# Linear attention with a folded FFN on one core: three transposes taken off TensorE

## What is computed

```python
q = _split_heads(x @ Wq.T + bq); k = _split_heads(x @ Wk.T + bk); v = _split_heads(x @ Wv.T + bv)
q = jnp.exp(q)
k = jnp.exp(k)
kv = jnp.cumsum(k[:, :, :, None] * v[:, :, None, :], axis=1)
k1 = jnp.cumsum(k, axis=1)
num = jnp.einsum('zsD,zsDd->zsd', q, kv)
den = jnp.sum(q * k1, axis=-1, keepdims=True)
att = merge_heads(num / den) @ Wo.T + bo
x1 = _layernorm(x + att)
h = x1 @ weight @ aux_weight1 @ aux_weight2
out = _layernorm(x1 + jnp.tanh(h + bias))
```

## Time and profile before

| | us |
|---|---|
| median of 3 runs | 2523.06 |
| lowest, highest | 2522.86, 2527.0 |
| the profiled execution | 2528.05 |
| its span, first to last instruction | 2526.3 |

### The profile page before, as it was taken

The page is one execution under the profiler, slowest core; times in us unless marked ns, Lnnn a source line. Parts: engine busy times, 40 slices in busy tenths (PEclk is TensorE's granted clock), DMA queues, the critical chain, the costliest instruction groups (busy, mean ns, idle before and its releaser), DMA issues.

```text
span 2526.3 us, 58437 instructions
## 1 busy us (share of the span) xinstructions
PE 2459.0 (97%) x22544; PEld 2082.3 (82%) x22544; DVE 1545.7 (61%) x2459; ACT 1070.2 (42%) x2156; POOL 1174.9 (47%) x1543
## 2 busy tenths in 40 slices
PE   7999999999999999999999999999999999999986
PEld 6788888888888888888888888888888888888875
DVE  4666656666566566656656666665665666666564
ACT  3434434444444444444444344444444444444432
POOL 0445444544454454444445445444544444454554
PEclk9999999999999999999999999999999999999997
DMA  4111111111111111111111111111111111111100
GB/s 158 39 45 45 39 42 48 39 39 51 39 39 43 47 39 39 51 39 38 47 43 39 41 49 39 39 50 40 39 43 47 39 39 47 43 38 43 35 30 26
DMA packets 59930, 111.99 MB, mean 44 GB/s; under 512 B 6720, under 2 KB 6720, under 8 KB 59712
## 3 DMA queue, kind: packets, MB, share of 16 engines
q1 hardware_dynamic: 59712, 108.56, 13.6%
HBM read 74.98 MB, written 33.55 MB: 43 GB/s over the span
## 4 chain that ended last, share of the span: by engine, by line
PE 96%; issue 2%; DVE 1%; ACT 0%; DMA 0%; POOL 0%; POOLq 0%; DVEq 0%; SPq 0%
PE G L273 19%; PE G L274 18%; PE G L275 18%; PE SC L340 6%; PE G L352 5%; PE SC L275 5%; PE SC L273 5%; PE SC L274 5%; PE G L329 4%; PE G L441 2%; PE G L424 2%; PE G L432 2%; PE G L361 1%; PE G L375 1%; PE G L376 1%
## 5 line engine op out<-in xcount | busy, mean ns | idle before, releaser
L721 POOL TENSOR_SCALAR_AFFINE_SELECT A<-A 128x512 f32<-128x512 f32 x512 | 313.8, 636 | 306.1 <-ACT A L495 306.1
L648 DVE RECIPROCAL o<-G 128x512 f32<-128x512 f32 x128 | 428.4, 3347 | 5.3 <-PE G L376 3.0
L495 ACT ACTIVATE A<-SC 128x512 f32<-128x512 f32 x512 | 278.5, 601 | 298.2 <-PE G L352 294.9
L530 ACT ACTIVATE QT<-G,bcol 128x512 f32<-128x512 f32 x128 | 88.3, 690 | 591.9 <-PE G L275 591.9
L755 POOL TENSOR_TENSOR qk1L<-WK,qk1H 128x512 fp32r<-128x512 f32 x128 | 163.2, 1275 | 342.4 <-ACT qk1H L535 342.4
L743 POOL TENSOR_SCALAR ve<-mv 128x1 f32<-128x1 f32 x128 | 28.5, 223 | 623.5 <-DVE mv L671 623.5
L643 DVE TENSOR_TENSOR WK<-G,bfbc 128x512 f32<-128x512 f32 x128 | 88.7, 693 | 300.1 <-PE G L275 300.1
L696 DVE TENSOR_TENSOR xTL<-G,xTH 128x512 fp32r<-128x512 f32 x128 | 88.5, 692 | 217.9 <-ACT xTH L543 217.8
L273 PE MATMUL G<-WfH,x1H 128*128 128x512 f32 x512 | 215.1, 420 | 1.6 <-DVE x1L L629 1.5
L635 DVE TENSOR_TENSOR o<-G,o 128x512 f32<-128x512 f32 x128 | 88.5, 692 | 196.0 <-PE G L352 195.9
L273 PE MATMUL G<-xTH,WkH 128*128 128x512 f32 x512 | 202.0, 394 | 5.9 <-DVE WkL L584 5.9
(11 more groups left out here) (113 smaller groups left out, 5747.1 us busy)
## 6 DMA issues: line engine op xcount, KB each, us to landing
xin<-x SPq DMA_DIRECT2D x128, 256.0 KB, 2.7
xres<-x SPq DMA_DIRECT2D x128, 256.0 KB, 2.6
out<-WK SPq DMA_DIRECT2D x128, 256.0 KB, 2.0
QT<-wqT SPq DMA_DIRECT2D x1, 1024.0 KB, 5.6
KT<-wkT SPq DMA_DIRECT2D x1, 1024.0 KB, 6.8
A<-a1T SPq DMA_DIRECT2D x1, 1024.0 KB, 7.8
WK<-a SPq DMA_DIRECT2D x1, 1024.0 KB, 10.0
WK<-wT SPq DMA_DIRECT2D x1, 1024.0 KB, 12.1
```

Source lines behind the costliest of these rows:

```text
L495: nc.scalar.activation(A[:, j, :, :].rearrange("p g q -> p (g q)"), SC[:, j, :], ACT.Copy).then_inc(scores_out[j], 1)
L648: nc.vector.reciprocal(oflat, den_ps[:, :]).then_inc(recip_ready, 1)
L721: last = nc.gpsimd.affine_select(out=A[:, j, :, :], in_=A[:, j, :, :], compare_op=ALU.is_ge, fill=0.0, base=0, pattern=[[0, NK], [1, P]], ...
```

## The change

The three transposes leave TensorE. For each, VectorE turns the 32x32 blocks of the 128x512 tile where they stand (`nc.vector.transpose`), and transfers put the blocks in their places. The identity matrix and the PSUM banks for the transposes go away.

- x: its load is now four transfers of 32 partitions each, which place the blocks at the load (`x_b`), and VectorE turns the blocks in place at the end of slot k for tile k+8. ScalarE makes xTH from that. The subtraction for xTL is now made by GpSimd, for tile k+7 in slot k, after the masks.
- K: VectorE turns the blocks into KS after the reciprocal, SyncE stores KS into a scratch tensor in device memory (`k_rows`), waits for it to land and loads Ktok back in four transfers.
- x1: SyncE stores x1 into a scratch tensor (`x1_rows`) and loads x1s back in four transfers; in the next slot VectorE turns the blocks of x1s into PSUM (bank 0 of SC, once the scores have been copied out of it), from where x1H and x1L are made.
- Order: on TensorE the FFN moves behind the output projection and the Q projection ahead of the K projection; V goes to the denominator's bank and waits for the reciprocal. On VectorE the second layer norm's statistics and scaling move into the next slot (tile k-3), and the addition for z is written into y directly. On GpSimd the addition for y and its inverse square root (tile k-3) open the slot. SyncE stores the output of tile k-3.
- Setup: Wq, Wk and Wv are loaded by blocks of 32 rows, and the FFN's first weight is permuted when it is split, so that the order of channels agrees.

The diff, cut to the slots (renaming, semaphores and setup left out):

```diff
+    x_b = x.rearrange("b (i t p) (a f) -> b i a p t f", t=P // HD, p=HD, a=HG)
+
+    k_rows = nc.dram_tensor("k_rows", [P, D], F32).ap()
+    x1_rows = nc.dram_tensor("x1_rows", [P, D], F32).ap()
+    k_blocks = k_rows.rearrange("(a p) (t c) -> t p a c", a=HG, t=HG)
+    x1_blocks = x1_rows.rearrange("(t p) (a f) -> a p t f", t=HG, a=HG)
...
+        state_ps, oproj_ps = G[1], G[1]
+        qproj_ps, ffn_ps = G[2], G[2]
+        den_ps, v_ps = G[3], G[3]
+        x1T_ps = SC[:, 0, :]
...
-                    wait_before(sp, (xtr_done, c.count(k + 7)))
                     n = k + 8
-                    sp.dma_start(xin[:, n % XIN, :], x_t[n % B, c.it + n // B]).then_inc(xin_loaded[n % B], 16)
+
+                    wait_before(sp, (xl_ready, c.count(n - 1)))
+                    for j in range(HG):
+                        sp.dma_start(xin[j * HD:(j + 1) * HD, n % XIN, :].rearrange("p (t f) -> p t f", t=HG),
+                                     x_b[n % B, c.it + n // B, j]).then_inc(xin_loaded[n % B], 16)
+                if c.exists(k - 3):
+                    n = k - 3
+                    wait_before(sp, (out_ready, c.count(n + 1)))
+                    sp.dma_start(out_t[n % B, c.it + n // B], y[:, n % 2, :]).then_inc(out_stored[n % B], 16)
...
+                if c.updates_state(k):
+                    wait_before(sp, (k_turned, c.count(k + 1)))
+                    sp.dma_start(k_rows, KS).then_inc(k_stored[k % B], 16)
+                    wait_before(sp, (k_stored[k % B], c.dma_count(k)), (state_done, c.count(k)))
+                    for j in range(HG):
+                        sp.dma_start(Ktok[j * HD:(j + 1) * HD, :].rearrange("p (a c) -> p a c", a=HG),
+                                     k_blocks[j]).then_inc(ktok_loaded[k % B], 16)
+                n = k - 1
+                if c.exists(n):
+                    wait_before(sp, (x1_ready, c.count(k)))
+                    sp.dma_start(x1_rows, x1[:, n % 2, :]).then_inc(x1_stored[n % B], 16)
...
+                    m = k + 1
+                    sp.dma_start(xres[:, m % 2, :], x_t[m % B, c.it + m // B]).then_inc(xres_loaded[m % B], 16)
+                if c.exists(n):
+                    wait_before(sp, (x1_stored[n % B], c.dma_count(n)), (x1_turned, c.count(n)))
+                    for j in range(HG):
+                        sp.dma_start(x1s[j * HD:(j + 1) * HD, :].rearrange("p (t f) -> p t f", t=HG),
+                                     x1_blocks[j]).then_inc(x1s_loaded[n % B], 16)
...
-                    wait(pe, ktok_ready, c.count(k))
+                    n = k - 1
+                    wait(pe, ktok_loaded[n % B], c.part_count(n))
+
+                    wait(pe, r_ready, c.count(n))
                     for g in range(NK):
                         for j in range(HG):
                             f0 = g * P + j * HD
                             last = nc.tensor.matmul(state_ps[j * HD:(j + 1) * HD, g * HD:(g + 1) * HD],
-                                                    Ktok[:, f0:f0 + HD], V[:, (k - 1) % 2, f0:f0 + HD],
-                                                    start=True, stop=True)
+                                                    Ktok[:, j * P + g * HD:j * P + (g + 1) * HD],
+                                                    V[:, n % 2, f0:f0 + HD], start=True, stop=True)
...
-                    wait(pe, xl_ready, c.count(k + 8))
+                    wait(pe, v_ready, c.count(k))
...
                     if not c.exists(k + 3):
+                        pe.wait_ge(wqh_ready, 1)
+                        pe.wait_ge(wql_ready, 1)
+                    wait(pe, xh_ready, c.quad_count(k + 4))
+                    wait(pe, xl_ready, c.quad_count(k + 4))
+
+                    wait(pe, z_ready, c.count(k - 2))
+                    wait(pe, q_ready, c.count(k + 4))
+                    three_pass(qproj_ps[:, :], lambda f: WqH[:, f, b * P:(b + 1) * P],
+                               lambda f: WqL[:, f, b * P:(b + 1) * P], lambda f: xTH[:, ns, f, :],
+                               lambda f: xTL[:, ns, f, :]).then_inc(qproj_done, 1)
...
+                if ffn:
+                    wait(pe, x1h_ready, c.count(k - 1))
+                    wait(pe, x1l_ready, c.count(k - 1))
+
+                    if proj:
+                        wait(pe, q_ready, c.count(k + 5))
+                    else:
+                        wait(pe, z_ready, c.count(k - 2))
+                    three_pass(ffn_ps[:, :], lambda f: x1H[:, f, :], lambda f: x1L[:, f, :],
+                               lambda f: WfH[:, f, :], lambda f: WfL[:, f, :]).then_inc(ffn_done, 1)
...
+                    wait(pe, recip_ready, c.count(k + 1))
...
-                if c.exists(k + 8):
-                    n = k + 8
-                    wait(pe, xin_loaded[n % B], c.dma_count(n))
-                    if att:
-                        wait(pe, recip_ready, c.count(k + 1))
-                    else:
-                        wait(pe, xl_ready, c.count(k + 7))
-                    for g in range(NK):
-                        last = nc.tensor.transpose(xtr_bank(c, k)[:, g * P:(g + 1) * P],
-                                                   xin[:, n % XIN, g * P:(g + 1) * P], ident[:])
-                    last.then_inc(xtr_done, 1)
-                if c.updates_state(k):
-                    wait(pe, r_ready, c.count(k))
-                    if not prev:
-                        wait(pe, xl_ready, c.count(k + 8))
-                    for g in range(NK):
-                        last = nc.tensor.transpose(ktr_ps[:, g * P:(g + 1) * P], KT[:, s, g, cols], ident[:])
-                    last.then_inc(ktr_done, 1)
-                if prev:
-                    wait(pe, x1_ready, c.count(k))
-                    if proj:
-                        wait(pe, q_ready, c.count(k + 5))
-                    else:
-                        wait(pe, z_ready, c.count(k - 1))
-                    for g in range(NK):
-                        last = nc.tensor.transpose(x1tr_ps[:, g * P:(g + 1) * P],
-                                                   x1[:, (k - 1) % 2, g * P:(g + 1) * P], ident[:])
...
                 if ffn:
-                    wait(act, z_ready, c.count(k - 1))
-                    nc.scalar.activation(z[:, :], z[:, :], ACT.Tanh).then_inc(tanh_ready, 1)
+                    wait(act, x1_turned, c.count(k - 1))
+                    wait(act, ffn_done, c.count(k - 2))
+                    nc.scalar.activation(x1H[:, :, :].rearrange("p g q -> p (g q)"), x1T_ps,
+                                         ACT.Copy).then_inc(x1h_ready, 1)
+                if proj:
+                    wait(act, qproj_done, c.count(k + 5))
+                    wait(act, num_done, c.quad_count(k - 4))
+                    nc.scalar.activation(QT[:, ns, b, :], qproj_ps[:, :], ACT.Exp,
...
+                    wait(act, x_turned, c.count(k + 9))
+                    wait(act, v_done, c.count(k + 1))
+                    nc.scalar.activation(
+                        xTH[:, (k // QUAD) % 2, :, b * P:(b + 1) * P].rearrange("p g (t q) -> p g t q", q=HD),
+                        xin[:, k % XIN, :].rearrange("p (t g q) -> p g t q", t=HG, q=HD),
+                        ACT.Copy).then_inc(xh_ready, 1)
...
+                if fin:
+                    wait(dve, y_ready, c.count(k - 2))
+                    nc.vector.bn_stats(bnst[:, 1, :], yf).then_inc(bn2_ready, 1)
+                    wait_before(dve, (bn2_ready, c.count(k - 2)), (rstd2_ready, c.count(k - 3)))
+                    nc.vector.bn_aggr(mv2[:, :], bnst[:, 1, :]).then_inc(stats2_ready, 1)
...
+                    n = k - 2
+                    wait(dve, x1s_loaded[n % B], c.part_count(n))
+
+                    wait(dve, scores_out[0], c.count(k + 1))
+                    nc.vector.transpose(x1T_ps.rearrange("p (g t q) -> p g t q", g=NK, q=HD),
+                                        x1s[:, :].rearrange("p (t g f) -> p g t f", t=HG, f=HD)).then_inc(x1_turned, 1)
+                if fin:
+                    wait(dve, rstd2_ready, c.count(k - 2))
+                    nc.vector.tensor_scalar(yf, yf, mv2[:, 0:1], rstd[:, 1:2],
+                                            ALU.subtract, ALU.mult).then_inc(out_ready, 1)
...
+                if c.updates_state(k):
+                    wait(dve, k_ready, c.quad_count(k))
+                    wait(dve, ktok_loaded[(k - 1) % B], c.part_count(k - 1))
+                    cols = slice(k % QUAD * P, (k % QUAD + 1) * P)
+                    nc.vector.transpose(KS[:, :].rearrange("p (t g f) -> p g t f", t=HG, f=HD),
+                                        KT[:, (k // QUAD) % 2, :, cols].rearrange("p g (t q) -> p g t q", q=HD)
+                                        ).then_inc(k_turned, 1)
...
+                if prev:
+                    wait(dve, rstd1_ready, c.count(k))
+                    wait(dve, y_ready, c.count(k - 2))
```

(55 more changed lines are left out.)

192 lines of the change are left out of this document (64 added, 128 removed).

## The result

| | before | after |
|---|---|---|
| median, us | 2522.96 | 2667.51 |
| lowest, highest | 2522.38, 2527.0 | 2663.78, 2675.72 |
| profiled span | 2526.3 | 2673.8 |
| TensorE, VectorE, GpSimd, ScalarE busy | 97%, 61%, 47%, 42% | 89%, 68%, 52%, 38% |
| mean granted TensorE clock | 0.991 | 0.952 |

The ratio is 1.057, with a 95% interval of 1.055 to 1.059. The direction was right; 2667 us lies above the range that ended at 2645.

A forecast was written before the change was run, and what follows sets the result against it. TensorE, busy 97% of the span, was taken as the bound. 2528.05 - 158.6 (transposes) + 172.1 (wait) + 49.6 (half clock) = 2591, less 5.0 from profiled time to median: 2586 us, range 2530 to 2645.

The forecast's parts named there:

- TensorE without its transposes: 363 groups of transposes leave TensorE's path at 0.437 us each: 158.6 us gained.
- wait for the low half of x: Q projection on TensorE waits 5.55 us for GpSimd's subtraction once in four slots, 31 times: 172.1 us lost.
- half clock behind it: TensorE's clock falls to half behind each 5.55 us gap: 1.6 us each, 31 times, 49.6 us lost.
- loop of x1 through device memory: x1's turn, engine work, store and loads across slots take 16.8 us, under TensorE's 17.61: costed at nothing.
- The gain: TensorE's slot falls from 18.92 to 17.61 us if nothing else comes late: 158.6 us in all.
- rival 1: Q projection's wait on xTL is absent or covered, GpSimd being through at 3.86 of the slot: 2364 us, chance 0.07.
- The wait: Q projection, asked for at 3.86 in every fourth slot, goes on at 9.41, behind GpSimd's masks and subtraction: 5.55 us.
- The clock: Half clock recurs behind each TensorE gap; 1.6 us each, from eight matmuls near the kernel's end, ends 0 and 2.6.
- Rival 2: The Q projection waits, but TensorE's clock doesn't fall or comes back at once: 2536 us, chance 0.15.
- why I cost it at nothing: Step on added VectorE transposes, x1's 16.8 us loop and SyncE's transfers: hidden by TensorE's slot, 0 us within 8.
- rival 3: x1's loop through device memory exceeds 19.4 us and sets the slot: 2725 us at 20.5 a slot, chance 0.13.
- Transposes and transfers: VectorE transposes take 0.65 us each, a store lands in 2.0 and a load in 2.7; GpSimd's subtraction takes 1.28.

The follow-up runs named there:

- run 8: Changed kernel with only VectorE's scaling of x1 moved ahead of the k1 copy and the product with Q; low half of x still late: 2603.33 us.
- run 5: Changed kernel with GpSimd's low half of x ahead of the masks and VectorE's scaling of x1 ahead of the k1 copy and product with Q: 2363.64 us.
- run 4: Changed kernel without x1's store and loads through device memory, block exchange left out (for timing only), low half of x still late: 2593.71 us.
- run 6: Changed kernel with the low half of x early and x1 not through device memory, its block exchange left out (for timing only): 2353.19 us.
- run 1: Changed kernel with GpSimd's subtraction for the low half of x moved ahead of the masks, right behind the addition for y: 2497.36 us.
- run 3: Changed kernel with one swap on ScalarE, V copied out of PSUM ahead of the tanh: 2671.12 us.
- run 9: Changed kernel with the scaling of x1 first, low half of x late, and 24 extra matmuls ahead of the Q projection's wait every fourth slot: 2551.74 us.
- run 10: Changed kernel with the low half of x early and GpSimd's qk1L made to wait until x1 is scaled, VectorE's order kept: 2364.11 us.

## Why the prediction was wrong, step by step

The runs split the change into four terms. The two of the late low half come together from run 8 less run 5 (239.7 us; run 4 less run 6 gives 240.5) and are told apart in run 8's trace, by the 31 distances from the last denominator matmul to the Q projection and from there to the K projection, each less what it is without a gap (0.23 and 2.75 us). Their sums, 173.3 and 66.9 us, add up to the 240.

| term | predicted | measured | from |
|---|---|---|---|
| TensorE without its transposes | -159 | -159 | run 5 (2363.6) against before (-162 against the before beside it) |
| wait for the low half of x | +172 (5.55 each) | +173 (5.6 each) | run 8 less run 5, by run 8's trace |
| half clock behind it | +50 (1.6 each) | +67 (2.2 each) | the same |
| loop of x1 through device memory | 0 | +64 | the changed kernel less run 8 |

- **The gain, right.** 2364 us was named as what the change would give with no wait at all (rival 1), and run 5 gave it. The match to a microsecond is luck in part: run 6, without x1's road, gains 170 us, and the road gives 10 of them back. Rival 1 itself was wrong for this kernel, since its condition, the subtraction ahead of the masks, was not met; run 1 and run 5 make it so.
- **The wait, right in place, cause, count and size.** TensorE's idle time is 5.4 us in the mean of run 8's 31 gaps, 5.6 from start to start. In the changed kernel it is 5.9, since the masks come later there; run 3 shows that its length grows with whatever makes them late.
- **The clock, right in kind, too small in size.** The half clock behind each gap cost 2.2 us in run 8 and 2.1 in the changed kernel, where the forecast took 1.6 and gave 2.6 as its upper end. The 1.6 was the loss of eight matmuls near the kernel's end; here most of the 12 matmuls of the Q projection ran slow. Filling the gap gave 64 us in the changed kernel. The Trainium skill ("TensorE: Matmul & The Clock Gate", HAM oscillation) was cited for the clock being paid behind each recurring wait; the runs agree, with 67 us for 31 waits.
- **Rival 2 (the clock stays), wrong** for the changed kernel; run 9, which keeps it by force, lies at 2552, where rival 2 had 2536.
- **The step that failed is "why I cost it at nothing"**: the loop of x1 was a term of 0 us and costs 64. It has two faults. First, the term for the loop was mis-sized: 16.8 us forecast, 18.5 and 19.2 read. VectorE's and GpSimd's part, from a turn to the store (1008.04 to 1020.22), is 12.2 us and not 10.9. The durations were taken from rows in which the two engines did not overlap in this way; in the new order the first step of the inverse root on GpSimd ran beside VectorE's product with Q (689 ns, and 221 ns in runs 5 and 8, where the order differs), and qk1L beside the scaling. The road from the store to the next turn took 6.1 to 7.1 us in four slots instead of 5.9 (6.4 in the median of all slots). Second, the comparison was wrong: the loop was set against TensorE's *average* slot, 19.4 us with the wait. But in three of four slots TensorE needs only 17.6, which the loop passed by about 1 us, and the long slot gives back only a part of the lateness collected there. With no long slot at all the loop costs 134 us (run 1 less run 5), with it 64: the cover that the prediction counted on hid about half. Behind the setup the short slots of the changed kernel take 18.0 us in the mean (17.7 in run 8), and its long slots 26.8 (25.4), so more than half of the loss is even paid in the long slot. So rival 3's threshold of 19.4 was too high; the right one was 17.6.
- **Transposes and transfers, right.** The turns take 0.65 to 0.73 us (forecast 0.65). A 64 KB load lands in 1.9 to 2.0 us and a store in 2.0. The subtraction read in runs of 32 elements took 1.28 to 1.31 us in the mean, by run, against 1.28 for the contiguous one. The exchanges of K and x are hidden, as run 6 shows.

Not taken further were where the last 10 us between run 5 and run 6 lie, and why the low half comes 0.6 us later when the gap is filled.

## What to carry to other kernels

When work leaves the busiest engine, follow each operand that it used to need early to its new place in the other engines' orders; a subtraction that ends some 6 us later in the slot (9.5 us into it in run 8, 3.5 in run 5) cost more than all the transposes saved. Compare a new loop through other engines and device memory with the shortest slot of the bounding engine and not with its average, since lateness adds up across short slots; here the average promised 0 us, 1 us over the shortest slot in all 128 would be 128, and it cost 64. And when VectorE and GpSimd orders are shuffled, take no duration over from the old trace until you know what will run beside it.

## What the runs showed of the hardware

- A 128x512 fp32 scaling on VectorE, SBUF to SBUF, took 547 ns alone and 1515 ns when a GpSimd subtraction of the same size started with it: it ended 0.3 us after the other. The Trainium skill says this in "SBUF — State Buffer" (Who interferes with whom): the two engines share a pair of ports, and a VectorE scaling in the two-port mode and a GpSimd instruction block each other fully, whichever came second. The trace agrees with the blocking, by the 0.3 us just named (no run shows the mode that the scaling was in), and run 10 shows what it can be worth: 133 us for one wait.
- A plain turn of 32x32 blocks of a 128x512 fp32 tile took 651 ns SBUF to SBUF (K; 695 ns for x, turned in place) and 727 ns into PSUM.
- Extra matmuls that compute nothing of use made a kernel 52 to 64 us faster by keeping the granted clock at 2.4 GHz across 31 gaps of 5.4 us (run 8) or 5.9 us (the changed kernel) in the mean.
- The Trainium skill's advice ("VectorE: DVE Perf Modes", Rules for kernel authors) to use TensorE for a 128x128 transpose where PSUM will do as destination did not hold here once the orders fitted: with TensorE the bound and both waits removed, the way over VectorE and transfers gave a ratio of 0.936 (run 5); with them it gave 1.057.
